# Weight conversions in pieces, residual rows one block ahead, norms ahead of bias additions

## The reference, cut to what matters

```
x = x + attn(layernorm(x))        # blocks of 128 rows, causal inside the block,
                                  #   D = H = 1024, out @ W_out.T + b_out
x = x + ffn(layernorm(x))         # ffn: two layers of
    h = shift_token(x); q, k, v = split(h @ wqkv)        # 8 heads of 64
    q, k = rotary_xpos(l2norm(q) * qs, l2norm(k) * ks)
    x = x + local_attention(q, k, v) @ wo                # window 512, looks one window back
    h = layernorm(shift_token(x)) * lg + lb
    a, g = split(h @ w1 + b1)                            # hidden size 2730
    x = x + (a * gelu(g)) @ w2 + b2
```

## Time and profile before

| | us |
|---|---|
| median of 3 runs (lowest, highest) | 4032.28 (4026.93, 4382.57) |
| the profiled execution, own time | 4015.77 |
| its span on the slowest core (core 1) | 4014.2 |
| spans of all cores | 3966.5 to 4014.2 |

### The profile page before, as it was taken

One profiled execution on the slowest core, in us unless ns is written; L12 is line 12 of the kernel. 1 busy time (PEld: TensorE's weight loads), 2 busy tenths in 40 slices (PEclk: granted clock), 3 DMA queues, 4 the chain that ended last, 5 costly groups with the idle time before them and its releaser, 6 DMA issues.

```text
span 4014.2 us, 55578 instructions; the slowest of 8 cores (3966.5 to 4014.2 us)
## 1 busy us (share of the span) xinstructions
PE 3407.0 (85%) x20890; PEld 1665.2 (41%) x20890; DVE 1395.9 (35%) x2537; ACT 884.8 (22%) x1328; POOL 1039.7 (26%) x881
## 2 busy tenths in 40 slices
PE   6888857888848789888998968888859999999998
PEld 3444423444424344343443534444424444444445
DVE  2455534555533122222222225455432222222221
ACT  1112113444421001110111114444501111111111
POOL 3344344434301111111111034334112212222112
PEclk9999978999979899999998988999979999999999
DMA  9434234687244421233113242342261111221112
GB/s 158 126 137 165 114 108 83 115 154 144 93 151 138 94 64 43 58 89 95 51 53 75 71 128 37 106 117 86 96 238 69 63 53 68 84 84 64 53 43 84
DMA packets 147063, 386.58 MB, mean 96 GB/s; under 512 B 12532, under 2 KB 47602, under 8 KB 146034
## 3 DMA queue, kind: packets, MB, share of 16 engines
q1 hardware_dynamic: 96578, 279.74, 19.8%
q0 software_dynamic: 36720, 70.26, 12.2%
q10 hardware_dynamic: 13504, 33.03, 2.4%
HBM read 342.10 MB, written 153.62 MB: 123 GB/s over the span
## 4 chain that ended last, share of the span: by engine, by line
PE 63%; DMA 11%; DVE 9%; POOL 7%; issue 4%; ACT 2%; ACTq 2%; SPq 1%; DVEq 0%; POOLq 0%
PE m_pu L60 30%; PE m_pd L60 9%; PE a_pr L60 9%; PE p_yp L60 3%; DMA m_xa<-xasp 3%; PE a_sc L60 3%; POOL m_xr L60 3%; PE p_qp L60 3%; DMA m_xr<-xbsp 2%; PE a_tb L60 2%; DVE a_t L60 2%; POOL a_qn L60 2%; ACTq L60 2%; PE a_av L60 1%; DMA m_xr<-xasp 1%
## 5 line engine op out<-in xcount | busy, mean ns | idle before, releaser
L60 PE MATMUL m_pu<-wA,m_w1b 128*128 128x512 bf16 (+2 forms) x4752 | 995.1, 370 | 0.0
L60 PEld LDWEIGHTS m_pu<-wA,m_w1b 128*128 128x128 bf16 x4752 | 462.6, 98 | 505.2
L60 ACT ACTIVATE wA<-m_pu,m_b1c 128x512 bf16<-128x512 f32 (+3 forms) x396 | 264.7, 669 | 1838.2 <-PE m_pu L60 1715.8
L60 PE MATMUL m_pd<-m_w,m_h 128*128 128x512 bf16 x2208 | 506.7, 381 | 31.8 <-DVE m_xr L60 31.8
L60 PE MATMUL a_pr<-wA,a_xT 128*128 128x512 bf16 x1776 | 467.7, 399 | 47.8 <-DVE a_t L60 37.5
L60 PE MATMUL m_pu<-wA,w1a 128*128 128x512 bf16 (+2 forms) x1440 | 336.1, 397 | 135.9 <-DVE m_h L60 134.3
L60 ACT ACTIVATE a_pT<-a_sc,a_nb 128x1024 bf16<-128x1024 f32 (+1 forms) x344 | 375.0, 1103 | 340.7 <-PE a_sc L60 338.9
L60 POOL TENSOR_TENSOR m_xr<-m_xr,m_b2r 128x1024 f32<-128x1024 f32 x69 | 161.8, 2345 | 1050.2 <-DMA m_xr<-xasp 559.3
L60 DVE SCALAR_TENSOR_TENSOR m_h<-m_pu,m_b1c,wA 128x512 bf16<-128x512 f32 (+2 forms) x288 | 208.4, 728 | 637.9 <-ACT wA L60 637.9
L60 PEld LDWEIGHTS m_pd<-m_w,m_h 128*128 128x128 bf16 x2208 | 212.4, 98 | 281.7 <-issue 43.8
L60 DVE TENSOR_TENSOR m_xr<-m_pd,m_xr 128x512 f32<-128x512 f32 x138 | 92.8, 689 | 568.8 <-POOL m_xr L60 426.3
(11 more groups left out here) (100 smaller groups left out, 3248.4 us busy)
## 6 DMA issues: line engine op xcount, KB each, us to landing
p_x<-xin SPq DMA_DIRECT2D x39, 512.0 KB, 6.7
xfsp<-p_xf SPq DMA_DIRECT2D x39, 512.0 KB, 2.9
a_xr<-xfsp SPq DMA_DIRECT2D x35, 512.0 KB, 8.0
xasp<-a_xr SPq DMA_DIRECT2D x35, 512.0 KB, 3.6
m_xr<-xasp SPq DMA_DIRECT2D x35, 512.0 KB, 4.3
xlsp<-m_xr SPq DMA_DIRECT2D x35, 512.0 KB, 3.3
a_xr<-xlsp SPq DMA_DIRECT2D x35, 512.0 KB, 5.6
xbsp<-a_xr SPq DMA_DIRECT2D x35, 512.0 KB, 3.0
```

The source lines that it names most:

```text
L60: ins = getattr(h, meth)(*args, **kw)
```

## The change

`narrow` becomes a generator that issues one transfer for each 128 rows (256 for `wo`): 8 for `qkv`, 2 for `wo`, 8 for each part of `w1`, 11 for each part of `w2`. In `phase1` the ten pieces are issued in one go. In layer 0's attention the 54 pieces are taken one after each step of the side generator once `gq > ga`. In layer 0's MLP the 64 pieces are taken one after every eighth product of `down`, from the second group on: 16 for each group of four blocks, so that the groups `gi` = 1 to 4 issue them all.

The residual rows get a function of their own. The first block's is called in `up` behind product pair 15, each further one in `down` between the two halves of the block before it.

In `phase1` a group's four norms are issued ahead of its four additions.

```diff
     def narrow(self, what, li, part):
         if what == "qkv":
-            out, in_ = self.sqkv[li], self.inp["fwqkv"][li]
+            out, in_, cuts = self.sqkv[li], self.inp["fwqkv"][li], range(0, D + 1, 128)
         elif what == "wo":
-            out, in_ = self.swo[li], self.inp["fwo"][li]
+            out, in_, cuts = self.swo[li], self.inp["fwo"][li], range(0, 513, 256)
...
         s = self.p.sem(self.es, f"sn_{what}{li}{part}")
-        self.narrowed[what, li, part] = self.p.emit("gpsimd", "dma_start", incn=16, inc=s, out=out, in_=in_)
+        for r0, r1 in zip(cuts[:-1], cuts[1:]):
+            self.narrowed[what, li, part] = self.p.emit("gpsimd", "dma_start", incn=16, inc=s,
+                                                        out=out[r0:r1, :], in_=in_[r0:r1, :])
+            yield 1
@@ phase1, prep
                 use.append(a)
-                b.full = op("gpsimd", "tensor_tensor", b.t[:], b.t[:], boutr[:], ALU.add, need=[a, t_bo])
-                yield 450
+                yield 150
+            for i, j in enumerate(blocks):
+                b = xr[j % 12]
+                b.full = op("gpsimd", "tensor_tensor", b.t[:], b.t[:], boutr[:], ALU.add, need=[use[i], t_bo])
+                yield 300
@@ attn
             for st_ in seq:
                 for c in st_:
                     yield c
+                if gq > ga:
+                    next(pieces, None)
...
-            if jobs:
-                self.narrow(*jobs.pop(0))
...
+        for _ in pieces:
+            pass
@@ mlp
                 out.append(v)
+                if pr == 15:
+                    residual(groups[gi][0])
...
+        def residual(j):
+            b = xr[j % 3]
+            ld = dma("sync", b.t[:], src[j * 128:(j + 1) * 128, :], f"xr{j % 3}",
+                     need=b.free + [src_tok[j]])
+            b.full = op("gpsimd", "tensor_tensor", b.t[:], b.t[:], b2r[:], ALU.add, need=[ld] + t_c)
+            if final:
+                r0 = (j - OWN_B) * 128
+                x1 = self.x1b
+                l1 = dma("sync", x1.t[:], self.x1sp[r0:r0 + 128, :], "xo", need=x1.free + [self.x1_tok[j]])
+                b.full = op("gpsimd", "tensor_tensor", b.t[:], b.t[:], x1.t[:], ALU.add, need=[l1, b.full])
+                x1.free = [b.full]
+
         def down(gi):
-            blocks = groups[gi]
-            for i, j in enumerate(blocks):
+            for i, j in enumerate(groups[gi]):
                 b = xr[j % 3]
-                ld = dma("sync", b.t[:], src[j * 128:(j + 1) * 128, :], f"xr{j % 3}",
-                         need=b.free + [src_tok[j]])
-                bb = op("gpsimd", "tensor_tensor", b.t[:], b.t[:], b2r[:], ALU.add, need=[ld] + t_c)
...
                         if kc % 8 == 7:
                             yield 1
+                            if gi > 0:
+                                next(pieces, None)
+                    if nh == 0 and i + 1 < len(groups[gi]):
+                        residual(groups[gi][i + 1])
                     o = b.t[:, nh * 512:(nh + 1) * 512]
-                    r = op("vector", "tensor_tensor", o, P.t[:, :], o, ALU.add, need=[t, bb])
+                    r = op("vector", "tensor_tensor", o, P.t[:, :], o, ALU.add, need=[t, b.full])
...
+        pieces = itertools.chain(*[self.narrow(*job) for job in jobs])
...
-            if jobs and gi > 0:
-                self.narrow(*jobs.pop(0))
             weave(both(gi), 43 + n * 6, side, 4400.0)
-        for job in jobs:
-            self.narrow(*job)
+        for _ in pieces:
+            pass
```

More of the change, by code:

```diff
@@ L1 @@
+import itertools
 import numpy as np
@@ L199, in narrow @@
         if what == "qkv":
-            out, in_ = self.sqkv[li], self.inp["fwqkv"][li]
+            out, in_, cuts = self.sqkv[li], self.inp["fwqkv"][li], range(0, D + 1, 128)
         elif what == "wo":
-            out, in_ = self.swo[li], self.inp["fwo"][li]
+            out, in_, cuts = self.swo[li], self.inp["fwo"][li], range(0, 513, 256)
         elif what == "w1":
             lo, hi = W1CUT[part] * 256, min(W1CUT[part + 1] * 256, W1C)
-            out, in_ = self.sw1[li][:, lo:hi], self.inp["fw1p"][li][:, lo:hi]
+            out, in_, cuts = self.sw1[li][:, lo:hi], self.inp["fw1p"][li][:, lo:hi], range(0, D + 1, 128)
         else:
             lo, hi = part * NCH * 64, (part + 1) * NCH * 64
-            out, in_ = self.sw2[li][lo:hi, :], self.inp["fw2p"][li][lo:hi, :]
+            out, in_, cuts = self.sw2[li][lo:hi, :], self.inp["fw2p"][li][lo:hi, :], range(0, NCH * 64 + 1, 128)
         s = self.p.sem(self.es, f"sn_{what}{li}{part}")
-        self.narrowed[what, li, part] = self.p.emit("gpsimd", "dma_start", incn=16, inc=s, out=out, in_=in_)
+        for r0, r1 in zip(cuts[:-1], cuts[1:]):
+            self.narrowed[what, li, part] = self.p.emit("gpsimd", "dma_start", incn=16, inc=s,
+                                                        out=out[r0:r1, :], in_=in_[r0:r1, :])
+            yield 1
     def load_attn_weights(self, queue, li, need):
@@ L579, in phase1 @@
         t_v.append(dma("gpsimd", h3_(tq[1], 0), wsrc("WvT", 1), "wq1", need=[rel[-1]]))
-        self.narrow("qkv", 0, 0)
-        self.narrow("wo", 0, 0)
+        for _ in itertools.chain(self.narrow("qkv", 0, 0), self.narrow("wo", 0, 0)):
+            pass
         state["wm"] = w
@@ L949, in attn @@
         jobs = [("w1", 0, 0), ("w1", 0, 1), ("w2", 0, 0), ("w2", 0, 1), ("w1", 0, 2), ("w1", 0, 3)]
-        jobs = jobs if li == 0 else []
+        pieces = itertools.chain(*[self.narrow(*job) for job in (jobs if li == 0 else [])])
         load(first + 1)
@@ L1166, in mlp @@
         if final:
-            self.x1b = [Buf(sb(pfx + f"x1b{i}", [128, D])) for i in range(1)] * 2
+            self.x1b = Buf(sb(pfx + "x1b", [128, D]))
         jobs = []
```

## The result

The ratio of the changed kernel's time to that of the kernel before is 0.972, with a 95% interval of 0.967 to 0.977. That is 2.8% faster, 113 us of 4032; the forecast was 98. The profiled execution went from 4015.8 to 3913.0 us, 103 less. The medians of four runs each are 3975.8 and 4151.2 us: they hold runs in which the cores of one die had a lower clock whatever the kernel, which the ratio leaves out, so they are no measure of the change.

A forecast was written before the change was run, and what follows sets the result against it. PE was taken to wait at MLP group borders for late residual additions and for `m_xa` loads sharing DMA engines with conversions. 37 + 56 + 9 - 5 + 1 = 98 us off 4015.8 gives 3918, as median 3934; range 3875 to 3995.

The forecast's parts named there:

- the level: Last step of the sum: 3918 us profiled plus 16.5, the median's distance above the profiled execution, gives 3934.
- the dip: PE's 16 products after a border wait take 5.30 us instead of 3.5; this 1.8 us loss was kept whole.
- One group undisturbed: MLP group of four blocks without disturbance: 114.2 us busy, 1.9 wait and 1.8 dip, 117.9 us in all.
- Residual rows ahead: MLP residual loads go 9.7 us earlier on SP, leaving 3.5 us of room, so rows are never late undisturbed.
- D: Rival: SP's order keeps residual rows from getting ahead; only three clean MLP borders gain, some 35 us, 3997; chance 0.04.
- Layer 0's MLP: Borders without a conversion save 56 us together; groups 1 to 4, with pieces, save 9 (bounds 44 saved, 49 lost).
- B: Rival: DMA engines stay the bound in layer 0's MLP groups 1 to 4, residual rows late; 53 saved, 3979; chance 0.21.
- A: Rival: the pieces disturb nobody, groups 1 to 4 are clean and attention loses nothing; 138 saved, 3894; chance 0.15.
- Attention, 5 us lost: Layer 0's attention: 48 more POOL issues at 0.735 us, 35 us over three groups; 5 lost, between 0 and 35.
- phase1, 1 us gained: Start of phase1: norms in a row remove PE's 2.65 us waits, but the fold needs weights; 1 gained (0 to 8).
- Rival C: Each piece holds the POOL queue for a fixed time, delaying attention's loads and MLP borders; 169 slower, 4201; chance 0.05.
- The rule on fixed time: Skill page's fixed 2.0 us per transfer: if it held the POOL queue, about 10 us saved in place of 98.

## Why the prediction was right and wrong

The mechanism held, and the sum of the terms is near what the profiled execution shows (98 us forecast, 103 there). Two steps were off: the level that turns the sum into a time, and the dip in the term for one group. That the sum comes out so close is in part luck. On core 1 the stages give 2 us in phase1, -9 in attention of layer 0, 70 and 51 in the two MLPs, and -6 in attention of layer 1, where nothing was changed: 108 in all. Only 103 are seen since another core, 7, is now the slowest.

- **The level.** The step that failed is the last of the sum, "the median of the runs shown is 16.5 us above that execution, and the same distance gives 3934". No run shows 16.5 us as a distance that a kernel keeps. With one more execution before's median became 4151.2, 135.4 us above its profiled one. The median of the changed kernel's four is 3975.8, 62.8 us above its own, and a fifth execution of 4078.4 moves it to 4031.3, beyond the range's 3995. What carries is the difference: 98 us, 2.4%, against 2.8% with an interval from 2.3 to 3.3%. Taken off before's 4032.3, the measured 2.8% give 3919.
- **One group undisturbed, 117.9 us.** Measured 116.0 in layer 1. The wait was right (1.73 to 2.16 us against 1.9). The dip of 1.8 us, kept whole, was not: behind none of the eight waits is there one. Seven periods times 1.9 are 13 us, and layer 1's MLP gained 49.3 where 37 were forecast. The term was mis-sized there, the mechanism right.
- **Residual rows ahead.** Right by itself: with them alone layer 1 has its whole gain, and no wait of PE on `m_xr` is left. So D falls.
- **Layer 0's MLP.** Forecast 65 (56 without pieces, 9 in groups 1 to 4) for core 1, whose stage went from 1183.6 to 1113.2, 70 less; the mean over the cores is 55 less, since core 1 had been the longest. By term, on core 1: group 0 saved 23.2 us (22.9 forecast), groups 1 to 4 11.5 (9), groups 5 and 6 29.2 (30.3), and the rest behind them 6.4 (3). The running order of POOL was foreseen to the piece. `m_xr` behind four pieces took 18.3, 15.9 and 14.7 us in groups 1 to 3, which the forecast had named as a sign of B, but together with waits of PE on PD, and there are none. The delay is paid at the border instead: in group 1 the last addition starts at 1464.34 us, 3.8 after PE has gone on to the next group (1460.53), where 0.3 is undisturbed. `m_xa` took 12.2, 13.3, 11.3 and 9.9 us at the four borders, 27.8 us over undisturbed in all, where 28.7 were forecast. So A falls (the four groups are not clean), and so does B (their loss is as forecast).
- **What the forecast had apart and is not.** It booked the three free borders to the conversions as a gain by themselves. The pieces alone gave 5 us: without the residual rows ahead, each stretched load is waited for. The 65 us hold only for both edits together.
- **Attention, 5 us lost.** 6.9 in the mean over the cores, and by what the experiments leave it is POOL's issues. The upper bound of 35 took 0.735 us for each, the price of an `a_xb` load; the pieces took half a microsecond. POOL is busy 24 us longer in the stage on core 1 (234.5 to 258.5), and over a quarter of that came through. Where these issues delay PE stays open: its wait on `a_qn` grows by 2 us in the three groups, and its own busy time over the stage goes from 503.9 to 506.3 us, and to 513.2 with 64-row pieces, as the mean granted clock goes from 0.92 to 0.91 and 0.90.
- **phase1, 1 us gained.** The norms alone start the fold 0.6 us earlier; in the stage nothing is to be seen.
- **Rival C's sum.** It takes attention's 5 us off a second time (98 - 5 - 205 - 57); without that it gives 164 slower, not 169. C falls either way: attention is 7 us longer, not 205.
- **The rule on fixed time.** The Trainium skill (DMA: Bandwidth & Descriptors, Anatomy of one DMA, SWDGE path) gives 2.0 us to each transfer and calls it mostly completion latency. In these runs it did not add up along the queue: 64 more transfers in the MLP cost no more than 3 us. No run here measures the 2.0 us by itself. Read as a latency, the page is not contradicted by the runs; read as a price per transfer in a busy queue, it is.

## What to carry to other kernels

Find out when a transfer is really issued: steps that stand evenly in a program come in bunches where the engine that issues them waits, and they should stand behind a wait that lies far from the next urgent load. Two causes that meet in one wait have to be removed together; either alone may show little or nothing. Small transfers cost time on the engine that issues them, so they belong there only where it is idle.

## What the runs showed of the hardware

- Six conversions of 2.5 to 3 MB, two at a time, kept the 16 DMA engines at a share of 1.02 from 640 to 830 us without delaying attention (631.5 us against 630.0). Its residual rows, tables and `a_xb` are issued a group ahead; loads of `a_xb` that landed up to 50.3 us after issue cost nothing.
- After waits of PE of 1.73 to 2.16 us the next 48 products took 10.52 us at all eight borders of the changed kernel's layer-1 MLP, with a granted clock of 1.00. In layer 0's, a wait of 2.37 us was followed by 12.21 us for 48 (granted clock 0.86), one of 3.05 by 10.52 (1.00), one of 13.32 by 12.37 (0.85). The loss of clock behind a wait does not follow its length in a simple way; what decides it stays open.
- A POOL-issued transfer takes POOL 0.49 to 0.6 us for a piece of 128 rows as for one of 64, so halving the pieces doubles POOL's time for issuing them.
